# A two-layer conditional conv and FFN kernel on one core: the setup before the first step is rebuilt, and two PE units of the main loop are moved by a row

## The reference

```python
# layer 0: eight expert 1x1 convolutions mixed per sample by an attention over `cond`, then a rank-128 FFN
h = gelu(gelu(cond @ W0 + b0) @ W1 + b1)
att = softmax(h @ W2 + b2)                                 # (128, 8)
agg_w = einsum('bk,koi->boi', att, weight)                 # (128, 64, 64): the "aggregated weights"
agg_b = att @ bias_k
y = einsum('boi,bih->boh', agg_w, x) + agg_b[:, :, None]
x = x + (einsum('bsd,od->bso', y, A @ B.T) + bias)
# layer 1: grouped 9-tap conv with a per-sample context, then a linear map with a top-1 LoRA expert
y = conv1d(x, weight, pad=4, groups=4) + (cond @ c_weight.T)[:, :, None] + fside_S_0[None, :, None]
x = x + y @ W_up.T + lora_of_top1_expert(y)
```

## Time and profile before

| | us |
|---|---|
| median of 3 runs (1112.57 to 1115.74) | 1114.72 |
| the profiled execution, its time | 1114.01 |
| its span, first to last instruction | 1112.2 |
| PE busy, DVE busy, ACT busy | 1081.2, 911.1, 605.3 |
| mean granted TensorE clock | 0.992 of 2.4 GHz |

### The profile page before, as it was taken

The page is one execution under the profiler, slowest core; times in us unless marked ns, Lnnn a source line. Parts: engine busy times, 40 slices in busy tenths (PEclk is TensorE's granted clock), DMA queues, the critical chain, the costliest instruction groups (busy, mean ns, idle before and its releaser), DMA issues.

```text
span 1112.2 us, 19139 instructions
## 1 busy us (share of the span) xinstructions
PE 1081.2 (97%) x7020; PEld 1050.3 (94%) x7020; DVE 911.1 (82%) x1670; ACT 605.3 (54%) x1243; POOL 4.3 (0%) x17
## 2 busy tenths in 40 slices
PE   6589999999999999999999999999999999999998
PEld 5488999999999999999999999999999999999998
DVE  6799888888878878888878888888887887888774
ACT  5666555555655545555555555555565554555441
POOL 1000000000000000000000000000000000000000
PEclk9699999999999999999999999999999999999999
DMA  8854445454445554445464444555445445543421
GB/s 323 244 120 131 119 116 148 151 144 140 114 122 137 144 160 129 116 116 140 143 158 135 140 111 117 147 151 150 133 114 122 138 144 160 131 123 90 112 58 77
DMA packets 118336, 152.03 MB, mean 137 GB/s; under 512 B 21868, under 2 KB 92268, under 8 KB 118092
## 3 DMA queue, kind: packets, MB, share of 16 engines
q1 hardware_dynamic: 116516, 148.36, 48.5%
q10 hardware_dynamic: 1728, 2.46, 0.7%
HBM read 80.87 MB, written 35.95 MB: 105 GB/s over the span
## 4 chain that ended last, share of the span: by engine, by line
PE 90%; DVE 4%; DMA 2%; SPq 1%; issue 1%; ACT 1%; DVEq 0%; ACTq 0%
PE M L1439 40%; PE H L1439 9%; PE G L1439 9%; PE F L1388 8%; PE F L1338 7%; PE F L1309 3%; PE F L1310 3%; PE F L1308 2%; PE M L1373 2%; PE G L1373 2%; PE M L1474 2%; SPq L349 1%; DMA x<-in_xP_dram 1%; PE F L1325 1%; PE F L1326 1%
## 5 line engine op out<-in xcount | busy, mean ns | idle before, releaser
L1439 PE MATMUL M<-Wsh,yh 128*128 128x384 f32 x896 | 308.1, 344 | 0.7 <-DVE yl L970 0.7
L1439 PE MATMUL M<-Wsl,yh 128*128 128x384 f32 x896 | 302.8, 338 | 0.0
L1439 PE MATMUL M<-Wsh,yl 128*128 128x384 f32 x896 | 302.1, 337 | 0.0
L919 DVE STREAM_TRANSPOSE yr<-F 128x512 f32<-128x512 f32 x126 | 90.1, 716 | 110.7 <-PE F L1388 110.7
L1439 PEld LDWEIGHTS M<-Wsh,yh 128*128 128x128 f32 x896 | 168.4, 188 | 4.2 <-DVE yl L970 1.0
L1439 PEld LDWEIGHTS M<-Wsl,yh 128*128 128x128 f32 x896 | 168.7, 188 | 2.7
L1439 PEld LDWEIGHTS M<-Wsh,yl 128*128 128x128 f32 x896 | 168.2, 188 | 0.0
L447 ACT ACTIVATE yh<-yr 128x1024 fp32r<-128x1024 f32 (+1 forms) x127 | 120.4, 948 | 20.1 <-DVE yr L934 14.9
L548 ACT ACTIVATE F<-G,cbX 128x128 f32<-128x128 f32 x252 | 70.2, 342 | 81.9 <-PE G L1373 81.9
L548 ACT ACTIVATE F<-M,cbX 128x128 f32<-128x128 f32 x260 | 72.3, 341 | 63.8 <-PE M L1373 63.8
L447 ACT ACTIVATE F<-biasb 128x512 f32<-128x512 f32 x124 | 74.5, 601 | 43.4 <-DVE yr L919 42.8
(11 more groups left out here) (199 smaller groups left out, 2538.4 us busy)
## 6 DMA issues: line engine op xcount, KB each, us to landing
x<-in_xP_dram SPq DMA_DIRECT2D x64, 516.0 KB, 4.3
xTr<-in_xT_dram SPq DMA_DIRECT2D x64, 512.0 KB, 3.7
Xr<-x SPq DMA_DIRECT2D x506, 64.5 KB, 2.5
out_dram<-x SPq DMA_DIRECT2D x62, 516.0 KB, 3.4
agb<-agb_scratch SPq DMA_DIRECT2D x31, 128.0 KB, 3.3
agg_scratch<-stage SPq DMA_DIRECT2D x1, 2048.0 KB, 9.5
agg<-agg_scratch SPq DMA_DIRECT2D x60, 32.0 KB, 3.2
Wsr<-in_Wsd_dram SPq DMA_DIRECT2D x2, 768.0 KB, 11.3
```

The lines of the kernel that those rows point to most:

```text
L919: dve.transpose(dst.rearrange("p j k m -> p (j k) m").rearrange("p (k r) (g b n) -> p g b k r n", r=2, g=2, b=4)[:, g % 2], F[g % 2][:, :] ...
L1439: last = pe.matmul(dst, w[:, y, k, :], m, start=fresh and n_ == 0, stop=k == 3 and n_ == 2, skip_group_check=True)
```

## The change

The setup and the hand-written part of step 0 are rebuilt; the loop has two units moved.

- **Attention and expert weights.** No split: the attention is transposed as it is (`attT`, 8 rows) and `agg_(c)`, `agb_small`, `agb_first` are plain fp32 products of it and `wkr`, now 8 rows, loaded once. `agg_(c)` has two banks (H and M2) in turn, so from the third on each waits for ACT's `evac(c-2)`; all eight `evac` are ACT's. The eight stand between other units on PE.
- **Step 0's aggregated weights.** `attb` spreads the attention of four samples over the partitions by two tiny fp32 matmuls with a selector, DVE's `prod` multiplies a second copy of the expert weights (`w0s`, 128x512, a new input of 256 KB) by it and `red` sums over the eight experts; ACT's `a0` puts the blocks in `agg`. The four `gg` transfers go.
- **B's sum** by three POOL additions and one matmul, `cb(g)` by ACT, `agg_out` in four transfers.
- **Conv of step 0.** No `unit_p`, no `xd`: X is split as it lies (`xh0`, `xl0`, 1032 columns each), and `unit_c(0, g)` has 12 matmuls in place of 6 that read every second column of it. ACT's `pc(0, g)` fills the bank from a zero tile and `cbX`.
- **Orders.** The three loads of B, expert weights and A are issued by ACT at its start, `x` of tile 0 is loaded early, the hand-written orders of PE, ACT, DVE and SP up to the loop are new, and row (0,0,0), the first big product (c0), stands ahead of `unit_o(1, 0)`.
- **Loop.** `unit_v(it+2)` and `unit_zt(2*it)` come after row 16 in place of 17, `unit_p(it+1, 0)` after row 18 in place of 19; `unit_u(it+3, 0)` stays after 19. The last two iterations keep theirs.

The core of the diff:

```diff
-            return slice(1024 * j, 1024 * j + (1024 if j < 3 else 1088))
+        AGB = (H, M[2])
...
             sp.dma_start(pack, mlp).then_inc(d_mlp, 16)
-            sp.dma_start(wkr[:, :], wkx).then_inc(d_wk, 16)
+            sp.dma_start(w0s[:, :, :], w0).then_inc(d_w0, 16)
             load_xT(0, 0)
             load_xT(0, 1)
-            sp.dma_start(Br[:, :, :], Bd).then_inc(d_b, 16)
+            load_x(0)
...
+            def a0():
+
+                act.wait_ge(v_a0, 1)
+                act.wait_ge(g_con, 4)
+                copy(agg[0:64, :, 0:64], agg0[0:64, :, :])
+                copy(agg[64:128, :, 64:128], agg0[64:128, :, :]).then_inc(a_a0, 1)
...
+            def xh0(q):
+                act.wait_ge(d_rx[q], 128)
...
+                copy((X0h, X0h2)[q][:, :, :], raw(0, q)[:, :, :]).then_inc(a_xs, 1)
...
+            def prod():
+
+                dve.wait_ge(d_w0, 16)
+                dve.wait_ge(p_at, 1)
+                dve.tensor_tensor(w0p[:, :, :, :], w0s[:, :, :].unsqueeze(1).broadcast_to([128, 2, C, 8]),
+                                  M[2][:, 0:16].rearrange("p (t k) -> p t k", t=2).unsqueeze(2).broadcast_to([128, 2, C, 8]),
+                                  ALU.mult).then_inc(v_pr, 1)
+
+            def red():
+                dve.wait_ge(v_pr, 1)
+                dve.tensor_reduce(agg0[:, :, :], w0p[:, :, :, :], AX.X, ALU.add).then_inc(v_a0, 1)
...
+                if s == 0:
+                    pe.wait_ge(v_t, 2)
+                    pe.wait_ge(v_xs, q + 1)
+                    h_, l_ = (X0h, X0h2)[q], (X0l, X0l2)[q]
+                    for e in range(2):
+                        for k in range(2):
+                            for n_, (w, m) in enumerate(((Th, h_), (Tl, h_), (Th, l_))):
+                                last = pe.matmul(dst[:, e], w[:, g, k, :], m[:, b0:b0 + 4, e + k:e + k + 127:2],
+                                                 start=False, stop=k == 1 and n_ == 2, skip_group_check=True)
...
             def agg_(c):
-                pe.wait_ge(v_wk, c // 2 + 1)
-                if c == 0:
-                    pe.wait_ge(v_mlp, 8)
-                if c == 7:
-                    pe.wait_ge(a_ag, 1)
-                pe.matmul(AGB[c][:, :], atsT[:, :], wks[:, 512 * c:512 * c + 512], start=True, stop=True).then_inc(p_ag, 1)
+                pe.wait_ge(v_mlp, 5)
+                pe.wait_ge(d_wk, 16)
+                if c > 1:
+                    pe.wait_ge(a_ag, c - 1)
...
+                pe.matmul(AGB[c % 2][:, :], attT[:, :], wkr[:, 512 * c:512 * c + 512], start=True, stop=True).then_inc(p_ag, 1)
...
-                    if n == 17 and not late:
+                    if n == 16 and not late:
                         unit_v(it + 2)
                         unit_zt(2 * it)
-                    if n == (16 if late else 19):
+                    if n == (16 if late else 18):
                         unit_p(it + 1, 0)
+                    if n == 19 + e:
                         unit_u(it + 3, 0)
-                    if n == 19 + e:
```

More of the change, by code:

```diff
@@ L702, in _ @@
+            bias(0, 0)
+            w21()
+            bias(0, 1)
+            w11()
+            ut(0)
+            bias(0, 2)
+            tuu(0)
+            a0()
+            agb_out()
+            txh(1, 0)
+            vhi(0)
+            txh(1, 1)
+            cb(0)
+            evac(1)
+            wc(0)
+            evac(2)
+            cb(1)
+            th()
+            cb(2)
+            evac(3)
+            lh()
+            rx0()
+            bias(0, 3)
             evac(4)
             evac(5)
+            cb(3)
@@ L704, in _ @@
+            w(0)
+            ut(1)
             evac(6)
             evac(7)
-            wc(0)
-            gg(0)
-            gg(1)
-            gg(2)
-            gg(3)
-            ah()
-            w11()
-            wc(1)
-            ut(0)
-            bias(0, 0)
-            bias(0, 1)
-            tuu(0)
-            lora()
-            txh(1, 0)
-            vhi(0)
-            bias(0, 2)
-            bias(0, 3)
-            th()
-            txh(1, 1)
-            lh()
-            w21()
@@ L727, in _ @@
[L727 to L745 removed]
+            xh0(0)
+            pc(0, 0)
+            w(1)
+            pc(0, 1)
+            tuu(1)
@@ L746, in _ @@
+            rx1()
+            w(2)
+            hA(0)
+            bias(1, 0)
+            vhi(1)
+            bias(1, 1)
+            pc(0, 2)
+            xh0(1)
+            pc(0, 3)
+            wc(1)
+            txh(2, 0)
             w(3)
-            pc(0, 3)
             cpGH(0)
+            w(4)
             bias(1, 2)
+            hB(0)
+            bias(1, 3)
             cpAB(0)
-            bias(1, 3)
-            hB(0)
             hC(0)
+            txh(2, 1)
             xs(1, 0)
-            txh(2, 1)
+            w(5)
@@ L1553, in _ @@
             row(0, 0, 3)
+            unit_c(0, 2)
             row(0, 1, 0)
-            unit_c(0, 2)
             unit_c(0, 3)
             row(0, 1, 1)
+            unit_u(2, 0)
             row(0, 1, 2)
@@ L1570, in _ @@
             row(0, 4, 3)
+            unit_o(1, 2)
+            unit_o(1, 3)
+            unit_u(2, 1)
             row(0, 3, 0)
+            unit_p(1, 0)
             row(0, 3, 1)
```

515 lines of the change are left out of this document (239 added, 276 removed).

## The result

The changed kernel took 1119.57 us (median of 10 runs, 1116.51 to 1121.45) against 1115.19 (10 runs, 1112.57 to 1116.01) of the kernel before beside it: ratio 1.0038, 95% interval 1.0025 to 1.0050. Submitted again in a later batch it gave 1.0038 (1.0024 to 1.0052). It is slower by 0.4%; the forecast of 1108.5 and its range to 1114.5 were wrong.

What follows compares the result with a forecast made beforehand. PE's own work bounds the loop, so setup gains move the end: -11.6 at row (0,0,0), +2.4 work and +4.0 idle give -5.2 (DVE -7.1), taken as -5.5; 1114.0 less 5.5 is 1108.5 us, range 1101.5 to 1114.5.

Steps and rivals of the forecast that it cites:

- half in I take 21 ... `unit_o(0, 0)` at 24.3: Setup: step 1's data lands at 21 us, so `unit_o(0, 0)` starts at 24.3, 7 us ahead of 31.25.
- the far bound of 23.4: Setup: time for all 7.9 MB on both queues at 337 GB/s; 5.95 MB would take 17.7 us.
- I cost them at nothing ... if that cover fails, 6.3 less the 1.5 is the price: Eight fp32 products on PE: hidden since PE waits for ACT's `evac` anyhow; otherwise 6.3 us against 1.5 before.
- the row of 2.05 us: Profile row of `cond`, four 128-column products in 2.05 us, read at 1.2 GHz to price the fp32 products.
- Sum 23.3, then `hA` itself: 47.0: From `vhi(0)` at 22.6, full ACT has 23.3 us of work, then `hA` takes 1.06 and ends at 47.0.
- 45.5 taken, 52.5 by the row: SP's queue: last `load_agg1` lands at 45.5, or 52.5 by the earlier 10.1 us landing; it decides from 48 on.
- my second rival (0.20): Late `evac` chain takes the gain: last `load_agg1` lands at 52.5, row (0,0,0) at 53, total 1113.3 us; chance 0.20.
- 48 matmuls at half rate cost 5.8 more, mostly beside ACT: Rival on step 0's conv: second-column reads at half rate cost 5.8 us more, giving 1112 to 1114; chance 0.07.
- Only at a third of the rate ... does it pass 1118: Same step 0 conv rival: passing 1118 us needs a third of the rate and the lower clock; chance 0.07.
- Behind row (0,0,0), +6.4: From row (0,0,0) to `unit_p(1, 0)`: part of the gain given back, 2.4 us of PE work plus 4.0 idle.
- my 4.0 of idle time: PE behind row (0,0,0): idle 4.8 us against 0.8 before, from waits of 2.8, 1.6 and 0.4.
- 1.5 us at most: Loop: moved units costed at nothing; an earlier `unit_p` ending a 0.05 us wait could gain this over 29 iterations.

Runs made afterwards that it cites:

- a5_start: Changed kernel with ACT's three early loads (B, expert weights, A) back on SP's queue and tile 0 of x behind `xT(1, .)`; ratio 1.0003 to the kernel before.
- a3_gg: Changed kernel with the four `load_agg1` and `load_agb(1)` ahead of the four `agg_out` on SP's queue; ratio 1.0042 to the kernel before.
- a1_loop: Kernel before with the loop's part of the change alone (`unit_v` and `unit_p` one row earlier, `unit_u` behind `unit_p`); ratio 0.9988, 1113.59 us.
- a2_planes: Changed kernel with step 0's X stored as planes of even and odd columns, so PE reads without a stride; ratio 1.0011 to the kernel before.
- d2_cold: Changed kernel with unstrided X, early loads on SP, SP's queue reordered, one `agg_out` transfer, step 1 and 2 splits earlier, no zero-adding matmuls; ratio 0.9995 to the kernel before.

## Why the prediction was wrong, step by step

- **"half in I take 21 ... `unit_o(0, 0)` at 24.3".** Landed 24.6, started 27.69; the terms between, 3.1 us, were right. The data was not at 21 but past the far bound of 23.4, as if all 7.9 MB had gone ahead of it: at the 324 GB/s of the window those are 24.4 us. The two issuers do share, as the Trainium skill has it (DMA: Bandwidth & Descriptors, Issuing engines are not separate DMA queues). ACT's early loads have a price besides: SP's issue of L380 took 3.25 us, where in a5_start it is 0.62 (there L382), and `mlp` landed at 5.1 instead of 4.1. Size: 3.4 us. a5_start gets 1.7 of it back at the landing and 0.3 at `unit_o(0, 0)`, so its 3.9 us are no measure of this term.
- **"I cost them at nothing ... if that cover fails, 6.3 less the 1.5 is the price".** This is the step that failed. "PE waits for ACT's `evac` of two banks anyhow" was an argument about one direction of a ring: with two banks, `evac(c)` waits for product c, which stands behind `unit_o`, `unit_u` and the product before it. PE was the slower side: ACT waited 3.07 us behind a stretch at the lower clock, and 0.91 even at the upper. The price of a product read from the row of 2.05 us came out (2.00 and 1.05, where I had 2 and 0.9), though by luck in one point: the view grants 1.00 at that row, and only the rate of the matmuls around it says that it ran at 1.2 GHz. The price that I named and dismissed, 4.8, was right too: the runs say 4.3.
- **"Sum 23.3, then `hA` itself: 47.0", ACT full.** ACT was busy 10.63 of 18 and 9.82 of 14 us. `hA` ended at 54.9, and waited 2.69 for DVE's transposes, that is for `unit_c(0, 0)` and `(0, 1)`: 24 matmuls of 0.23 from 47.25 on (5.5 us), which stood in no sum since I laid the whole conv under ACT.
- **"45.5 taken, 52.5 by the row".** Landed at 55.70, 10.2 later: 8.2 from the last `evac`, 1.2 from SP's issues behind it (6.9 us to the last of them, where I had 5.7) and 0.8 from a landing of 3.95. That row (0,0,0) hung on it was my second rival (0.20), right in place; a3_gg shows that it was not what the time hung on.
- **"48 matmuls at half rate cost 5.8 more, mostly beside ACT".** Half rate was right at the upper clock, 0.23 for 0.12, and the half of the matmuls that stands there costs 2.6 on the path; at the lower clock the stride costs 0.016 us each. "Only at a third of the rate ... does it pass 1118" left out that this loss could come with others; it had 0.07.
- **Behind row (0,0,0), +6.4.** Right in size for the wrong reasons: row (0,0,0) was 1.3 ahead, `unit_p(1, 0)` 6.4 behind before (81.64 to 75.24), so 7.7 were given back. Of my 4.0 of idle time 0.97 and 0.72 came; the rest is 2.6 of strided reads and 1.2 of six 512-column matmuls at 0.43 in place of 0.23, the clock being low until 62.2.
- **The loop.** Costed at nothing, "1.5 us at most": 1.8 by the marks, of which the moved units show 0.3.

Sum by the rows: row (0,0,0) -1.3 instead of -11.6, then +7.7, which makes +6.4 at `unit_p(1, 0)`; 1.2 of it comes back ahead of the loop's first `unit_v`, so setup +5.2, loop -1.8: +3.4, 1117.4 for that execution. What stays open is why the changed kernel's loop is 0.05 us shorter per iteration beyond what a1_loop shows, where those 1.2 us come back, why the clock falls at 23 us in one execution and at 28 in another, and how the gain of each single repair divides between time on the chain and the clock: the edits overlap, and no run holds the clock still.

## What to carry to other kernels

Idle time of an engine that falls is no gain if the work that fills it is slower: follow the chain, not the busy share. Before a product is costed at nothing because its consumer frees the bank late, walk the ring both ways, and at the lower clock too: here PE was at it for 10 us in one execution and 17 in the other, in the middle of the setup's chain. Before a mark that moved between two traces is put down to an edit, compare where the clock fell in each. Where the setup's chain leads through in-order queues, each repair moves the wait to the next late transfer; sum what single repairs gain only after running two together.

## What the runs showed of the hardware

- A matmul of 256 fp32r columns that reads every second fp32 column starts 0.229 us after the one before it, at the lower and at the upper clock (changed kernel); without the stride it is 0.213 and 0.12 (a2_planes).
- The same program differed by 2.10 us between two executions with a granted clock of 0.72 and 0.55 from 24 to 42 us; 0.43 of it was a later landing ahead of that. In the slower one the clock fell while PE was busy, not behind a gap.
- Twelve matmuls that add zeros, put in a gap of 3.2 us, delayed what follows by 3.4 us, brought the upper clock back at 31 instead of 38 us, and made the kernel 3.0 us faster. With the gap gone (d2_cold) they give 0.7, not told from none.
